# A two-layer kernel whose second mixture of experts is computed on sorted rows in 46 blocks instead of densely

## The reference, cut to what matters

```python
def _L1_ffn_ref(x, Wg, W1, W2, W3):
    E = 8
    TOP_K = 2
    DIM = 128
    HID = 256
    xf = x.reshape(-1, C)
    logits = xf @ Wg
    top_w, top_i = jax.lax.top_k(logits, TOP_K)
    top_w = jax.nn.softmax(top_w, axis=-1)
    ...
    h = jnp.einsum('nc,ech->enh', xf, W1)
    g = jnp.einsum('nc,ech->enh', xf, W2)
    y = jnp.einsum('enh,ehc->enc', jax.nn.silu(h) * g, W3)
    out = jnp.einsum('enc,ne->nc', y, combine)
    ...
x = _layernorm(x + _L1_attn_ref(...), axis=-1)
x = _layernorm(x + _L1_ffn_ref(...), axis=-1)
```

## Time and profile before

| | |
|---|---|
| median of 3 runs | 850.84 us (850.53 to 855.11) |
| the profiled execution | span 846.4 us from its first to its last instruction; no time of its own is listed beside it, so the 4.4 us between the span and the median are taken as what lies around the span |
| first instruction of the second attention's matmuls | 500.0 us |
| first matmul of the second feed-forward part | 686.9 us |
| busy over the whole span | PE 677.3, DVE 674.4, ACT 493.2, POOL 127.6 us |
| DMA queues used | SP's and ACT's only; GpSimd issues none |

### The profile page before, as it was taken

The page is one execution under the profiler, slowest core; times in us unless marked ns, Lnnn a source line. Parts: engine busy times, 40 slices in busy tenths (PEclk is TensorE's granted clock), DMA queues, the critical chain, the costliest instruction groups (busy, mean ns, idle before and its releaser), DMA issues. The chain is left out here.

```text
span 846.4 us, 14707 instructions
## 1 busy us (share of the span) xinstructions
PE 677.3 (80%) x5386; PEld 537.2 (63%) x5386; DVE 674.4 (80%) x1432; ACT 493.2 (58%) x893; POOL 127.6 (15%) x101
## 2 busy tenths in 40 slices
PE   6376675756658979999999956787886889999996
PEld 4265564645556757877778843454553468888886
DVE  3999899999985997988979857788887256868765
ACT  4667667687555664777856822677765444333232
POOL 1112212131403760010010029000000000000000
PEclk9568788677678988999989975899998589999999
DMA  7354334344423610303002031000000000000000
GB/s 233 91 155 115 100 88 114 107 125 128 123 72 85 197 26 1 100 1 101 0 1 101 1 95 54 1 2 1 2 2 1 1 1 1 1 13 1 14 14 13
DMA packets 76699, 48.30 MB, mean 57 GB/s; under 512 B 54994, under 2 KB 64980, under 8 KB 76628
## 3 DMA queue, kind: packets, MB, share of 16 engines
q1 hardware_dynamic: 73268, 44.75, 18.2%
q10 hardware_dynamic: 3360, 2.62, 1.0%
HBM read 37.85 MB, written 9.50 MB: 56 GB/s over the span
## 5 line engine op out<-in xcount | busy, mean ns | idle before, releaser
L983 ACT ACTIVATE hT<-hps,b1s 128x512 f32<-128x512 f32 x128 | 88.2, 692 | 63.6 <-PE hps L897 61.6
L1148 DVE TENSOR_TENSOR hl<-hT,hh 128x512 fp32r<-128x512 f32 x128 | 96.4, 776 | 23.8 <-ACT hh L989 22.4
L1592 DVE TENSOR_REDUCE mx<-s_ps 128x2 f32<-128x512 f32 x128 | 82.4, 686 | 27.9 <-PE s_ps L1351 27.9
L1820 ACT ACTIVATE act_h<-up 128x512 f32<-128x512 f32 x64 | 38.3, 598 | 89.2 <-PE up L1774 89.2
L1525 ACT ACTIVATE pt<-st_ps 128x512 f32<-128x512 f32 x128 | 69.7, 599 | 34.1 <-PE st_ps L1361 33.2
L320 ACT ACTIVATE rest<-rest,par 128x264 f32<-128x264 f32 x128 | 53.7, 502 | 36.2 <-DVE rest L591 36.2
L313 ACT ACTIVATE tap<-cst_s,par 128x328 f32<-128x328 f32 x128 | 72.3, 652 | 3.8 <-DVE par L644 3.8
L1902 DVE TENSOR_TENSOR hid<-act_h,up 128x512 f32<-128x512 f32 x64 | 43.3, 685 | 28.1 <-PE up L1774 17.0
L1785 PEld LDWEIGHTS eo<-wc,hid 128*128 128x128 f32 x512 | 61.7, 192 | 2.4
L1785 PE MATMUL eo<-wc,hid 128*128 128x128 f32 x512 | 62.1, 275 | 0.0
L1351 PE MATMUL s_ps<-kf,qf 32*128 32x256 f32 x256 | 35.4, 354 | 32.3 <-DVE mx L1592 28.7
(11 more groups left out here) (340 smaller groups left out, 1692.4 us busy)
## 6 DMA issues: line engine op xcount, KB each, us to landing
kd<-kst SPq DMA_DIRECT2D x16, 512.0 KB, 2.6
xc<-in_x_coarse SPq DMA_DIRECT2D x16, 512.0 KB, 4.1
wdB<-wdd SPq DMA_DIRECT2D x32, 256.0 KB, 6.0
dW<-kd SPq DMA_DIRECT2D x16, 256.0 KB, 3.4
Ks<-kd SPq DMA_DIRECT2D x64, 33.0 KB, 2.1
dW<-kd SPq DMA_DIRECT2D x64, 32.0 KB, 2.1
w1r<-in_w ACTq DMA_DIRECT2D x5, 256.0 KB, 2.9
w2r<-in_w ACTq DMA_DIRECT2D x5, 256.0 KB, 3.3
```

Of the source, the lines that this page charges most:

```text
L983: nc.scalar.activation(hT[k][:], hps[:, k, :], ACT.Gelu, bias=b1s[:, m:m + 1]).then_inc(h_done, 1)
L1148: nc.vector.tensor_tensor(hl[s % 2][:, k, :], hT[k][:], hh[s % 2][:, k, :].bitcast(F32), ALU.subtract).then_inc(hl_done, 1)
L1592: nc.vector.tensor_reduce(mx[:, :, h:h + 1], s_ps[k][:].rearrange("p (t k) -> p t k", t=2), AX, ALU.max).then_inc(s_used, 1)
```

## The change

The second feed-forward part computes only the pairs of token and expert that are used. The 2048 tokens are taken in two halves, A and B (`Route`), 1024 tokens or 8 tiles of 128 each. For a half, the kernel computes the logits, the two chosen experts, and for each token its two positions in a list sorted by expert, in which each expert's share is rounded up to blocks of 128 slots: 23 blocks hold it whatever the choice, 46 for both halves. The counting is done by small matmuls with a triangular matrix (`route_prefix`) and VectorE operations (`route_ends`, `route_slots`, `route_owners`). GpSimd scatters the rows of `xs_all` to a list `xd` in HBM by 16 indirect DMAs per half (128 rows of 512 bytes each); SP loads them back in chunks of 4 blocks. For each block TensorE turns the rows, multiplies them as the fixed operand with 512 columns of [W1 W2] of the block's expert in one float32 matmul, turns the two halves of the result and multiplies them with W3 in two float32 matmuls. The column where the expert's weights begin in `wres` comes from a register that TensorE loads from SBUF, four blocks at a time. Results go to a list `yd` in HBM, and GpSimd gathers them back by 16 indirect DMAs per half, before `route_pair` adds them with their shares and takes the statistics. `xd` is set to zero by two DMAs in the second attention; the splitting of the expert weights is gone. Half A's routing stands in rounds 8 and 9 of the attention and its scatter at the end of GpSimd's queue in that block; half B's routing stands in the first blocks of the last part.

```diff
@@ finish, second attention, gpsimd
-            pool.wait_ge(ffn1_in, 64)
-            for high, full in ((wah, wa), (wbh, wb)):
-                last = nc.gpsimd.tensor_copy(flat2(high[:]), flat2(full[:]))
...
+            for R in routes:
+                route_zero(nc, R)
+            pool.wait_ge(ffn1_rows, 32)
+            route_scatter(nc, pool, routes[0], xs_all, xd[0])
@@ tensor
+                if i == B:
+                    route_turned(nc, pe, routes[0], xs_all, s_ps, ident)
                 if i == B + 1:
...
+                    route_prefix(nc, pe, routes[0], s_ps[1], tri)
...
+                if i == B:
+                    pe.wait_ge(ffn1_in, 48)
+                    route_logits(nc, pe, routes[0], s_ps[0], wgs)
@@ scalar
-                if i == B + 1:
-                    act.wait_ge(sqrt0_go, 1)
-                    nc.scalar.activation(vv0[:], vv0[:], ACT.Sqrt).then_inc(sqrt0_done, 1)
+                if i == B:
+                    route_root(nc, act, routes[0])
@@ last part, sync: load(c) brings 4 blocks of xd, store(i) writes 2 blocks of yd
+                sp.wait_ge(routes[g].scattered, 32 * routes[g].n)
...
+            for c in range(3):
+                load(c)
+            for i in range(len(PAIRS)):
+                if i % 2 == 0 and i // 2 + 3 < len(CHUNKS) and i >= 2:
+                    load(i // 2 + 2)
+                store(i)
...
@@ gpsimd
+            route_scatter(nc, pool, second, xs_all, xd[1])
+            for i in range(pairs_in(0) - 3, pairs_in(0)):
+                pool.wait_ge(eos_out[i % 3], 16 * (i // 3 + 1))
+            route_gather(nc, first, yd[0])
...
+            for i in range(len(PAIRS) - 3, len(PAIRS)):
+                pool.wait_ge(eos_out[i % 3], 16 * (i // 3 + 1))
+            route_gather(nc, second, yd[1])
@@ tensor
+            def up(j):
...
+                if at % 4 == 0:
+                    _, found = nc.values_load_multi_w_load_instructions(
+                        routes[g].eb[0:1, at:at + 4], min_val=0, max_val=(E - 1) * WROW, engines=[nc.tensor.engine])
...
+                nc.tensor.matmul(up_ps[j % 2][:], xsT[pair_of[j] % 2][:, at_pair[j], :], wres[:, bass.ds(owners[g, at], 2 * HID)],
+                                 start=True, stop=True).then_inc(up_ready, 1)
...
+            route_turned(nc, pe, second, xs_all, rt_ps, ident)
+            rows_turned(0)
+            for j in range(TOTAL + 2):
+                if j < TOTAL:
+                    if opens(j) and pair_of[j] + 1 < len(PAIRS):
+                        rows_turned(pair_of[j] + 1)
+                    up(j)
+                if j >= 2:
+                    down(j - 2)
+                if 1 <= j <= TOTAL:
+                    hidden_turned(j - 1)
+                if j == 0:
+                    route_logits(nc, pe, second, rt_ps[0], wgs)
+                if j == 4:
+                    route_prefix(nc, pe, second, rt_ps[1], tri)
@@ new functions
+def route_scatter(nc, pool, R, x, rows):
...
+    for t in range(R.n):
+        for k in range(2):
+            nc.gpsimd.indirect_dma_start(out=rows, out_offset=bass.IndirectOffsetOnAxis(ap=R.pos[:, t, k:k + 1], axis=0),
+                                         in_=x[:, R.first + t, :], in_offset=None).then_inc(R.scattered, 16)
+def route_pair(nc, v, link, R, x, m):
...
+    v.wait_ge(R.gathered[m], 64)
+    for k in range(2):
+        for t in range(2 * m, 2 * m + 2):
+            row = x[:, R.first + t, :]
+            last = nc.vector.scalar_tensor_tensor(row, R.got[:, t, k, :], R.pr[:, t, k:k + 1], row, ALU.mult, ALU.add)
```

More of the change, by code:

```diff
@@ new lines, in tiles_of, with route_zero, route_variances @@
+def tiles_of(ap):
+    return ap[:].rearrange("p t e -> p (t e)")
+def route_zero(nc, R):
+    nc.gpsimd.memset(R.run[:], 0.0)
+    nc.gpsimd.memset(R.count[:, R.n, :], 0.0).then_inc(R.zeroed, 1)
+def route_variances(nc, link, R, x):
+    for t in range(R.n):
+        last = nc.vector.bn_stats(R.stats[:, t, :], x[:, R.first + t, :])
+    link(last)
+    for t in range(R.n):
+        last = nc.vector.bn_aggr(R.mv[:, t, :], R.stats[:, t, :])
+    link(last)
+    nc.vector.tensor_scalar(R.vv[:], R.mv[:, :, 1], EPS, None, ALU.add).then_inc(R.var_set, 1)
@@ new lines, in route_root, with route_rows, route_turned @@
+def route_root(nc, act, R):
+    act.wait_ge(R.var_set, 1)
+    nc.scalar.activation(R.vv[:], R.vv[:], ACT.Sqrt).then_inc(R.root_done, 1)
+def route_rows(nc, v, link, R, x):
+    v.wait_ge(R.root_done, 1)
+    link(nc.vector.reciprocal(R.rs[:], R.vv[:]))
+    for t in range(R.n):
+        row = x[:, R.first + t, :]
+        last = nc.vector.tensor_scalar(row, row, R.mv[:, t, 0:1], R.rs[:, t:t + 1], ALU.subtract, ALU.mult)
+    last.then_inc(R.rows_set, 1)
+def route_turned(nc, pe, R, x, banks, ident):
+    pe.wait_ge(R.rows_set, 1)
+    for t in range(R.n):
+        last = nc.tensor.transpose(banks[t // 4][:, t % 4 * P:(t % 4 + 1) * P], x[:, R.first + t, :], ident[:])
+        if t % 4 == 3:
+            last.then_inc(R.turned, 1)
@@ new lines, in route_prefix, with route_shares @@
+def route_prefix(nc, pe, R, bank, tri):
+    pe.wait_ge(R.count_set, 1)
+    pe.wait_ge(R.zeroed, 1)
+    full = (R.n + 1) * E
+    nc.tensor.matmul(bank[:, 0:full], tri[:, 0:P], tiles_of(R.count), start=True, stop=False)
+    for s in range(1, R.n + 1):
+        last = nc.tensor.matmul(bank[:, s * E:full], tri[:, P:2 * P], tiles_of(R.count)[:, 0:full - s * E],
+                                start=False, stop=(s == R.n))
+    last.then_inc(R.prefix_ready, 1)
+def route_shares(nc, v, R):
+    v.wait_ge(R.th_done, 1)
+    nc.vector.tensor_scalar(R.pr[:, :, 0:1], R.th[:], 0.5, 0.5, ALU.mult, ALU.add)
+    nc.vector.tensor_scalar(R.pr[:, :, 1:2], R.th[:], -0.5, 0.5, ALU.mult, ALU.add)
@@ L168, in build @@
             dve = sem("g_dve")
+            used = range(ld_first.num, dve.num + 1)
             block = ctx.enter_context(nc.Block())
@@ L1637, in _ @@
             split(1)
[L1638 to L1653, removed]
             for i in range(ROUNDS):
@@ L1723, in finish @@
+        eos_out = [sem(f"eos_out{u}") for u in range(3)]
+        y_ready = sem("y_ready6")
         dve = sem("dve6")
@@ new lines, in _ @@
+            route_root(nc, act, second)
+            nc.scalar.activation(warm[:], eps_t[:], ACT.Silu)
+            share(first)
+            rows_copied(0)
+            for j in range(TOTAL + 2):
+                if j < TOTAL:
+                    silu(j)
+                    if opens(j) and pair_of[j] + 1 < len(PAIRS):
+                        rows_copied(pair_of[j] + 1)
+                if 1 <= j <= TOTAL:
+                    hidden_copied(j - 1)
+                if j == 3:
+                    share(second)
+                if j == NB + 18:
+                    root(first, 2)
@@ L1837, in _ @@
+            root(second, 2)
         @block.vector
@@ L1960 @@
+            for m in range(second.n // 2):
+                link(route_pair(nc, v, link, second, xs_all, m))
+            ends(second)
+            inverse(second)
+            for k in range(HALVES):
+                rows_out(second, 1, k)
+            v.wait_ge(y_ready, 2 * HALVES)
 def kernel(**inputs):
```

562 lines of the change are left out of this document (303 added, 259 removed).

## The result

| | median | ratio to before, 95% interval |
|---|---|---|
| before | 852.0 us (850.53 to 855.11, 4 runs) | |
| after | 862.37 us (861.71 to 863.48, 4 runs) | 1.0119 [1.0096, 1.0141] |

The forecast was 846.0 us, 0.6% faster; the change costs 1.2%. The profiled execution of the changed kernel took 862.56 us with a span of 860.6. The page of the profile shows what became of the last part (busy time, then tenths in 40 slices, and the group of `up` matmuls).

The account below looks back on a forecast made before the run. The last part was taken as bound by TensorE's matmuls. Terms placed along the span, with 32 exposed indirect DMAs, reached 841.6 us, and 4.4 us around the span made 846.0 us; range 822 to 875, the forecast's own 841 to 856.

Parts of the forecast that it names:

- positions of half A known: End of the attention: routing in rounds 8 and 9 done at 688.2 us, or 693.8 with 5.6 us added in round 8.
- scatter A: Between attention and last part: 16 indirect DMAs that nothing covers, 16.0 us, ending at 709.8 us.
- barrier: Between attention and last part: waits for GpSimd's queue, then 0.3 us, so the last part starts at 710.1 us.
- start of the last part to first `up`: Half B's statistics, root, rows and turns ahead of the first block: 8.4 us, hiding the sorted rows' load; first block at 718.5.
- blocks: Last part: 46 blocks at TensorE's pace of 1.64 us, 75.4 us; with extras and drain 95.1 us, to 813.6.
- gathers B: Tail behind the last result: 16 gathers with nothing beside them, 16 us, from 816.2 to 832.2 us.
- s: GpSimd's queue time per indirect DMA: 1.0 us, between 0.5 (SP's spacing) and 2.1 (landing); span 809.6 + 32 s.
- The register loads: TensorE's queue in the blocks: 12 loads with 8 register instructions each, 0.65 us apiece, 7.8 in all (bounds 0 and 13.7).
- the cold start: First two blocks of the last part: TensorE at 1.2 GHz after waiting, 2.5 us extra.
- both middle rows of DMAs: During the blocks: GpSimd's scatter of half B and gather of half A, both hidden with s = 1.0.
- rival 2: Indirect DMAs hold GpSimd's queue longer, above 1.28 us each; at 2.1 us the time is 881 us. Chance 0.20.
- rival 4: Blocks miss TensorE's pace: 0.4 us hand-over waits per block give 864 us, or a clock of 0.83 gives 861. Chance 0.11.

Follow-up runs that it names:

- e5_rows: Changed kernel with each scatter and gather DMA cut to the first 64 partitions' rows, others left out: 862.6 us, 1.0161 of the kernel before.
- e2_early: Changed kernel with each register load right behind the previous block's `up` product, the first ahead of the first rows' turning: 851.4 us, 1.0005 of the kernel before.
- e3_moved: Changed kernel with the first half's scatter moved from the attention's end to the start of the last part's GpSimd row: 859.2 us, 1.0085 of the kernel before.
- e1_static: Changed kernel with constant expert addresses in place of register loads, so blocks may use the wrong expert: 850.7 us, 0.9978 of the kernel before.

## Why the prediction was wrong

The sum ran to 841.6 us on the span's clock; the span ended at 860.6. Term by term:

| term | predicted | measured | difference |
|---|---|---|---|
| positions of half A known (end) | 693.8 | 692.2 | -1.6 |
| hand-over to the first DMA | 0 | 0.9 | +0.9 |
| scatter A | 16.0 | 20.1 | +4.1 |
| barrier | 0.3 | 2.2 | +1.9 |
| start of the last part to first `up` | 8.4 | 11.9 | +3.5 |
| blocks | 95.1 | 101.2 | +6.1 |
| copy and store of the last result | 2.6 | 2.6 | 0 |
| gathers B | 16.0 | 19.8 | +3.8 |
| landing, pair, rows, store | 9.35 | 9.6 | +0.3 |

**The step that failed** is the one on which the prediction said that everything hangs, s, the time that one indirect DMA holds GpSimd's queue. It was set at 1.0 us, the geometric middle of 0.5 and 2.1, and is 1.26 for the scatter and 1.25 for the gather: 7.9 of the 19 us, enough alone to turn 0.6% faster into 0.4% slower. The other 11 us are the terms below. The reason for placing it there was wrong as well: "128 addresses to fetch" put it above SP's row, but e5_rows shows that 64 addresses less save 0.07 us. The mechanism was right, with 32 such DMAs exposed. The Trainium skill, "DMA: Bandwidth & Descriptors" (the section on the anatomy of one DMA), has 2.0 us plus the bytes at 436 GB/s for one DMA issued by GpSimd; 2.15 us is the estimate from it for the 64 KB of one here. The 2.2 us from a scatter's issue to its landing agree with it, the 2.5 of a gather are above it. It is no price of the queue: the next DMA starts 1.26 us behind the last, ahead of its landing.

**The register loads** were the second mis-sized term: 0.65 us each (7.8), with bounds of 0 and 1.14. In the blocks a group of four takes 1.24 us more than the parts of its blocks, which is above the upper bound; eleven of them are 13.6 us. e2_early, which moves nothing else, gave 8.4 of them back. That the short turns cover them was only half right: some 0.8 us of results and turns lie beside the load, but the load with its register instructions holds the sequencer for 1.5 us, and the product behind the idle time is longer by 0.26. The twelfth load, 1.24 us ahead of the first `up`, had not been seen as part of that path. "Runtime: NRT & Kernel Launch" of the Trainium skill (instruction fetch mechanics) has 200 ns per register loaded from HBM. Here one load of four from SBUF took 330 ns, less than the 0.8 us worked out from it; the register instructions behind it, 0.66 us and 0.5 of gaps, are what that figure does not hold.

**The start of the last part**: the products, statistics and rows have the sizes given. Missing were the table load for silu and its warming call (1.5 us), behind which the shares of half A and so VectorE's whole row stood, the register load, and some 0.6 of small steps.

**The barrier**: 0.3 was taken and 2.2 came, counted from the end of the last scatter DMA (also in the two runs with constants and with early loads, 712.86 to 715.07 and 711.96 to 714.17). e3_moved, with no DMA of GpSimd under way there, has the 0.3. So the 1.9 us more are the price of a scatter right ahead of the barrier. It is argued, not shown, that the barrier waits for the DMAs to land: the last one landed at 714.5, 1 us before the next part began.

**What held**: the positions of half A, 1.6 us sooner than forecast, though that point moves by 9 us between executions, so that so close a hit is in part luck; TensorE's pace in the blocks (three blocks in four at 1.52 to 1.74 us, 1.64 predicted); the clock, 0.95 over the blocks and 1.00 in e2_early's (725 to 813), so that the turns did it no harm that could be seen; the cold start, 3.1 us for the first three `up` where 2.5 stood; both middle rows of DMAs hidden; the tail behind the gathers within 0.3 us. The logits and counting of half B took 5.1 us for 4.0, as the logits ran at half the clock. `route_pair` did stop VectorE (3.0 foreseen, at four places), but the steps of TensorE there are those of their neighbours but for one, 3.34 us for 2.88, ahead of the product at 812.69: it costs some 0.5 us. The table loads for half A's root, not in the sum, stand on the chain at 818; the steps there are longer by about 0.5 us in all.

**The base**: 4.4 us had been put around the span from a median of other executions. The profiled execution after shows 2.0, so a span of 841.6 would have been 843.6. The profiled execution before was a quick one, too: the two spans lie 14.2 us apart, the medians 10.4.

None of the rivals won as it stood. The slower side was right, but s of 1.26 lies within the forecast's own 0.85 to 1.3 and under the 1.28 from which rival 2 decides. The measured 862.4 us are near rival 4's 861 and 864, but not by its mechanism: the clock was 0.95, and blocks without a load kept TensorE's pace. It was each term a little above its middle: seven terms of nine were too small and one too large.

## What to carry to other kernels

Count the indirect DMAs that nothing covers, by instruction and not by row, at 1.26 us each (128 rows of 512 bytes), and put other work of the next part beside them; a barrier between the two parts forbids that. Where a kernel reads a value into a register of a busy engine, write the load right behind a long instruction, which then runs beside it, and not behind short ones: for twelve loads of 1.5 us each that was worth some 10 us here. When a sum has many unseen terms, take the next part's first microseconds row by row (table loads, first register load), since these are what a sum from the old trace leaves out.

## What the runs showed of the hardware

- An indirect DMA of 128 rows of 512 bytes holds GpSimd's queue for 0.96 us and a gap of 0.30; with 64 rows it is 0.89. A scatter DMA lands 2.2 us after its issue, one of the last gather 2.4 to 2.6 (the changed kernel).
- A load of four registers from SBUF takes TensorE's sequencer 0.33 us, the register instructions behind it 0.66 and the gaps between them 0.5, 1.5 us in all; a matmul whose operand is addressed by a register is not slower than one with a constant address (0.86 us in e2_early and in e1_static).
- A barrier behind a row of GpSimd's scatter DMAs ended 2.2 us after the last of them had left the queue (the changed kernel), one without them 0.3 us after the last instruction (e3_moved).
- Programs that are the same up to the end of the attention differ by up to 9 us there, with the granted clock ahead of it at 0.53 to 0.74. Counted from that point, two executions of the changed kernel agree to the tenth (168.6 and 168.6 us), but the clock can differ behind it too: in e2_early by 4.5 us.
